# Mask of layer 3 added on VectorE with the row extremum, no mask products on TensorE, logits left in PSUM, all lists in a new order

## The reference

```
scores = einsum('bhqd,bhkd->bhqk', q, k) * scale
scores = where(adj == 0, -inf, scores)
attn = softmax(scores)
out = einsum('bhqk,bhkd->bhqd', attn, v) @ Wo.T + bo
```

## Time and profile before

| | us |
|---|---|
| median of 3 runs (lowest, highest) | 1394.55 (1393.59, 1395.53) |
| profiled execution, its own time | 1394.57 |
| its span in the trace | 1392.7 |
| mean granted TensorE clock, share of full | 0.994 |
| VectorE busy in TENSOR_REDUCE (L497, 256 of them) | 170.7 |
| VectorE busy in masked reductions (L450, 256) | 138.0 |
| ScalarE busy in layer 3's exponentials (L676, 1024) | 362.7 |

### The profile page before, as it was taken

How to read it: one execution, slowest core, us unless ns; L and a number is a source line. 1 busy time by engine, 2 the same in 40 slices (tenths; PEclk the granted TensorE clock), 3 DMA queues, 4 the chain that set the end, 5 groups by cost and what they waited for, 6 DMA issues and landing times. The chain is left out here.

```text
span 1392.7 us, 41293 instructions
## 1 busy us (share of the span) xinstructions
PE 1341.1 (96%) x12689; PEld 1173.4 (84%) x12689; DVE 1077.8 (77%) x3934; ACT 1006.3 (72%) x3905; POOL 918.3 (66%) x1225
## 2 busy tenths in 40 slices
PE   2799999999999999999999999999999999999986
PEld 2588888888888888888988888888888888898875
DVE  3787787787787788788778778778778778877853
ACT  0367777777777777777777777777777777777765
POOL 1577667677676776776776766767667677676543
PEclk9999999999999999999999999999999999999999
DMA  3001001101101001101000110110110110110000
GB/s 102 22 17 32 30 19 32 32 17 32 32 17 32 32 17 32 32 17 32 32 25 25 32 32 18 32 32 17 32 32 17 32 32 17 32 32 17 10 17 24
DMA packets 38888, 38.89 MB, mean 28 GB/s; under 512 B 3088, under 2 KB 38672, under 8 KB 38672
## 3 DMA queue, kind: packets, MB, share of 16 engines
q1 hardware_dynamic: 38672, 36.26, 8.5%
HBM read 19.47 MB, written 16.78 MB: 26 GB/s over the span
## 5 line engine op out<-in xcount | busy, mean ns | idle before, releaser
L301 POOL TENSOR_TENSOR probs<-exps,rsum 128x512 f32<-128x512 f32 x256 | 263.6, 1041 | 185.3 <-DVE rsum L504 185.3
L676 ACT ACTIVATE exps<-bank,nmax 128x128 f32<-128x128 f32 x1024 | 362.7, 383 | 1.7 <-DVE nmax L497 1.7
L441 DVE SCALAR_TENSOR_TENSOR ht_lo<-bank,ht_hi 128x512 fp32r<-128x512 f32 x192 | 130.8, 681 | 260.1 <-ACT ht_hi L614 260.1
L273 POOL TENSOR_TENSOR rstd<-veps,power 128x2 f32<-128x2 f32 x256 | 177.1, 692 | 212.8 <-DVE veps L412 212.7
L281 POOL TENSOR_SCALAR y<-x,nm,rstd 128x256 f32<-128x256 f32 x512 | 278.9, 554 | 33.0 <-issue 31.6
L684 ACT ACTIVATE probs3t<-bank 128x512 f32<-128x512 f32 x256 | 162.0, 634 | 103.1 <-PE bank L880 103.1
L676 ACT ACTIVATION_READ_ACCUMULATOR exps<-bank,nmax 128x1 f32 x1024 | 229.2, 224 | 0.0
L766 PE MATMUL bank<-w_hi,ht_hi 128*128 128x512 f32 (+1 forms) x512 | 185.9, 363 | 5.5 <-DVE ht_lo L441 5.4
L396 DVE BATCH_NORM_STATS2 stats<-x 128x6 f32<-128x256 f32 x512 | 186.7, 404 | 0.1
L768 PE MATMUL bank<-w_hi,ht_lo 128*128 128x512 f32 (+1 forms) x512 | 174.9, 342 | 0.0
L767 PE MATMUL bank<-w_lo,ht_hi 128*128 128x512 f32 (+1 forms) x512 | 174.3, 341 | 0.0
(11 more groups left out here) (121 smaller groups left out, 3786.7 us busy)
## 6 DMA issues: line engine op xcount, KB each, us to landing
x<-in_x SPq DMA_DIRECT2D x64, 256.0 KB, 2.8
out<-x SPq DMA_DIRECT2D x64, 256.0 KB, 3.1
w_sb<-in_w0t SPq DMA_DIRECT2D x1, 512.0 KB, 4.6
w_sb<-in_w SPq DMA_DIRECT2D x1, 256.0 KB, 5.2
w1t_sb<-in_w1t SPq DMA_DIRECT2D x1, 256.0 KB, 5.2
wq_sb<-in_wqt SPq DMA_DIRECT2D x1, 256.0 KB, 3.8
wk_sb<-in_wkt SPq DMA_DIRECT2D x1, 256.0 KB, 4.1
wv_sb<-in_wvt SPq DMA_DIRECT2D x1, 256.0 KB, 4.4
```

The lines of the kernel that those rows point to most:

```text
L273: pool.tensor_tensor(rstd[i][:, b], veps[i][:, b], power[:], ALU.pow).then_inc(S[f"rstd{i}"], 1)
L301: pool.tensor_tensor(probs3[:, p % BUFFERS["probs3"], j], exps3[:, p % BUFFERS["exps3"], j], rsum3[:, s, j].unsqueeze(2).to_broadcast([P, ...
L676: last = act.activation(exps3[:, b, j, i], bank_of(f"sc{j}")[:, i * P:(i + 1) * P], ACT.Exp, bias=nmax3[:, s, j, i:i + 1], accum_out=ssum3 ...
```

## The change

- The four mask products per pair go, with `start_scores`; `scores` begins its banks itself and now waits for all four.
- On VectorE `mask_scores` takes the place of `score_maximum`: per 128x128 score tile one TENSOR_TENSOR_REDUCE adds the mask, writes the negated sum to the new SBUF tile `masked3` (one buffer) and leaves its minimum in `nmax3`; four per bank, sixteen per pair. It waits for the exponentials of the pair before.
- `exps3_of` reads `masked3` with scale -1 in place of the bank. The score banks are freed by `nmax3_j`, no longer by `exp3_j`.
- `sum_logits` of layers 1 and 2 writes the logits into the other half of their PSUM bank, and `mask_logits` reads them there and writes `z`; the banks `d1` and `d2` are freed by `nmax1` and `nmax2`.
- The fp32 staging copies of six weights lie in `exps3` and `probs3`.
- The lags, the banks and the order of all four engines' lists are new. In the new table of lags the operations of each engine stand in the order of its new list.

The diff, cut to its core (the written-out lists of `step` follow the order of the new `LAG`; of `BANKS` the new table alone):

```
-       "load": -4, "store": 4, "e1t": 2, "qt_mm": 4, "x2_mm": 2, "mask3": 4, "e2t": 3, "mask1": 4, "scores": 4, "x3_mm": 3, "pt0": 5, "m1": 0,
-       "ot_mm": 5, "h1t": 1, "m0": 0, "x4_mm": 5, "v_mm": 4, "wh1_mm": 1, "wh0_mm": 1, "h2t": 2, "h3t": 3, "pt3": 4, "s0": 0, "pt2": 4, "d1": 1,
-       "hh_mm": 2, "kt_mm": 3, "d2": 2, "mask2": 3, "h0t": -1, "pt1": 4, "mask0": 3, "mj_hi0": 0, "exp3_0": 4, "wh1": 1, "exp3_1": 4, "wh0": 1,
-       "ht2": 2, "h3t_hi": 3, "v": 4, "p3t_2": 4, "z1": 1, "hh": 2, "p3t_3": 4, "exp1": 1, "z2": 2, "h0t_hi": -1, "at1": 1, "exp2": 2, "at2": 2,
-       "p3t_1": 4, "p3t_0": 4, "exp3_3": 3, "mj_hi1": -1, "ot_hi": 4, "h1t_hi": 0, "exp3_2": 3, "rsum3_0": 4, "stats1": 0, "kt": 3, "rsum1_any": 1,
-       "mv1": 0, "nmax2": 2, "veps1": 0, "h0t_lo": -1, "qt": 3, "rsum1": 1, "mv0": -2, "rsum2": 2, "x2": 1, "veps0": -2, "stats2": 1, "nmax3_3": 3,
-       "mv2": 1, "x3": 2, "veps2": 1, "nmax3_2": 3, "stats3": 2, "nmax3_0": 3, "mv3": 2, "t0_1": -1, "veps3": 2, "ot_lo": 4, "h1t_lo": 0,
-       "mj_lo1": -1, "rsum3_3": 3, "nmax3_1": 3, "mj_lo0": -1, "rsum3_2": 3, "t0_0": -1, "x4": 4, "h3t_lo": 2, "rsum3_1": 3, "stats0": -3, "x1": -1,
-       "nmax1": 0, "p3_1": 4, "x3_tail": 2, "p3_0": 4, "r3": 3, "rstd1": 0, "y1": 0, "rstd0": -2, "rstd2": 1, "y2": 1, "rstd3": 2, "y3": 2, "p3_3": 3,
-       "p3_2": 3, "y0": -2, "r0": -3,
+       "load": -4, "store": 5, "m1": 0, "pt3": 5, "v_mm": 4, "ot_mm": 5, "wh1_mm": 1, "wh0_mm": 1, "s0": 0, "h2t": 2, "d1": 1, "h0t": -1, "h3t": 3,
+       "pt2": 4, "x4_mm": 5, "hh_mm": 2, "kt_mm": 3, "e1t": 1, "d2": 2, "qt_mm": 3, "x2_mm": 1, "pt1": 4, "scores": 3, "m0": -1, "e2t": 2, "pt0": 4,
+       "h1t": 0, "x3_mm": 2, "p3t_0": 5, "mj_hi0": 0, "h1t_hi": 1, "exp3_3": 4, "mj_hi1": 0, "p3t_3": 5, "exp3_2": 4, "v": 4, "ot_hi": 5, "wh1": 1,
+       "wh0": 1, "z1": 1, "ht2": 2, "h3t_hi": 3, "h0t_hi": -1, "exp3_1": 4, "exp1": 1, "hh": 2, "at1": 1, "z2": 2, "exp3_0": 4, "exp2": 2, "p3t_2": 4,
+       "p3t_1": 4, "at2": 2, "stats2": 2, "nmax3_3": 4, "nmax3_0": 4, "mv2": 2, "nmax3_2": 4, "veps2": 2, "x3": 3, "h1t_lo": 1, "stats3": 3,
+       "mj_lo0": 0, "mv3": 3, "mj_lo1": 0, "veps3": 3, "t0_1": 0, "t0_0": 0, "nmax3_1": 4, "rsum3_2": 4, "ot_lo": 5, "x1": 0, "stats1": 0, "nmax1": 1,
+       "mv1": 0, "h3t_lo": 3, "veps1": 0, "h0t_lo": -1, "stats0": -3, "mv0": -3, "x4": 5, "rsum3_1": 4, "rsum1_any": 1, "kt": 3, "nmax2": 2, "qt": 3,
+       "rsum1": 1, "veps0": -3, "rsum3_0": 4, "x2": 1, "rsum3_3": 4, "rsum2": 2, "r0": -1, "rstd1": 1, "p3_1": 5, "x3_tail": 3, "y1": 1, "p3_0": 5,
+       "r3": 4, "rstd0": -2, "p3_3": 5, "rstd2": 2, "y2": 2, "rstd3": 3, "y3": 3, "p3_2": 4, "y0": -2,
 }
 
 
...
 BANKS = {
+    "m1": (4, "m1", ('mj_lo1', 't0_1')),
+    "pt3": (2, "pt3", ('p3t_3',)),
+    "v": (0, "v_mm", ('v',)),
+    "ot": (3, "ot_mm", ('ot_lo',)),
+    "wh1": (7, "wh1_mm", ('wh1',)),
+    "wh0": (0, "wh0_mm", ('wh0',)),
+    "x1b": (2, "s0", ('x1',)),
+    "h2t": (7, "h2t", ('ht2',)),
+    "d1": (5, "d1", ('nmax1',)),
+    "h0t": (6, "h0t", ('h0t_lo',)),
+    "h3t": (0, "h3t", ('h3t_lo',)),
+    "pt2": (4, "pt2", ('p3t_2',)),
+    "x4b": (3, "x4_mm", ('x4',)),
+    "hh": (2, "hh_mm", ('hh',)),
+    "kt": (5, "kt_mm", ('kt',)),
     "at1": (1, "e1t", ('at1',)),
+    "d2": (7, "d2", ('nmax2',)),
+    "qt": (0, "qt_mm", ('qt',)),
+    "x2b": (2, "x2_mm", ('x2',)),
+    "pt1": (7, "pt1", ('p3t_1',)),
+    "sc0": (3, "scores", ('nmax3_0',)),
+    "sc1": (1, "scores", ('nmax3_1',)),
+    "sc2": (0, "scores", ('nmax3_2',)),
+    "sc3": (5, "scores", ('nmax3_3',)),
+    "m0": (6, "m0", ('mj_lo0', 't0_0')),
+    "at2": (4, "e2t", ('at2',)),
+    "pt0": (2, "pt0", ('p3t_0',)),
     "h1t": (5, "h1t", ('h1t_lo',)),
+    "x3b": (7, "x3_mm", ('x3',)),
...
+        masked3 = sb("masked3", [P, BUFFERS["masked3"], HPC, DC * G, P])
...
+        w0_sb = probs3[:, 0, 0:2].rearrange("p j b n -> p (j b n)").rearrange("p (c o) -> p c o", o=D)
+        w1t_sb = probs3[:, 0, 2].rearrange("p b n -> p (b n)").rearrange("p (c o) -> p c o", o=D)
+        wq_sb, wk_sb, wv_sb, wo_sb = [exps3[:, 0, j].rearrange("p b n -> p (b n)").rearrange("p (c o) -> p c o", o=D) for j in range(HPC)]
...
             def mask_logits(i, msk, p):
                 b, s = p % BUFFERS[f"z{i}"], p % SMALL
                 passed(dve, f"z{i}", p)
                 passed(dve, f"exp{i}", p, SMALL)
-                for g in range(G):
-                    last = dve.tensor_tensor_reduce(z[i][:, b, g], z[i][:, b, g], msk[:], scale=-1.0, scalar=-MASKED, op0=ALU.add, op1=ALU.min,
+                read_before(dve, f"z{i}", p, f"exp{i}")
+                for g in range(G):
+                    last = dve.tensor_tensor_reduce(z[i][:, b, g], bank_of(f"d{i}")[:, (G + g) * P:(G + g + 1) * P], msk[:], scale=-1.0, scalar=-MASKED, op0=ALU.add, op1=ALU.min,
                                                     accum_out=nmax[i][:, s, g:g + 1])
                 last.then_inc(S[f"nmax{i}"], 1)
...
-            def score_maximum(j, p):
-                s = p % SMALL
+            def mask_scores(j, p):
+                b, s = p % BUFFERS["masked3"], p % SMALL
                 passed(dve, "scores", p)
-                passed(dve, f"exp3_{j}", p, SMALL)
-                dve.tensor_reduce(nmax3[:, s, j], bank_of(f"sc{j}")[:].rearrange("p (b n) -> p b n", n=P), AX.X, ALU.max,
-                                  negate=True).then_inc(S[f"nmax3_{j}"], 1)
+                passed(dve, f"exp3_{j}", p, BUFFERS["masked3"])
+                for i in range(DC * G):
+                    last = dve.tensor_tensor_reduce(masked3[:, b, j, i], bank_of(f"sc{j}")[:, i * P:(i + 1) * P], mask[:], scale=-1.0, scalar=-MASKED,
+                                                    op0=ALU.add, op1=ALU.min, accum_out=nmax3[:, s, j, i:i + 1])
+                last.then_inc(S[f"nmax3_{j}"], 1)
 
...
             def sum_logits(i, src, buffer, col, p):
-                b, bs = p % BUFFERS[f"z{i}"], p % BUFFERS[buffer]
+                bs = p % BUFFERS[buffer]
                 passed(act, f"d{i}", p)
-                read_before(act, f"z{i}", p, f"exp{i}")
-                for g in range(G):
-                    last = act.activation(z[i][:, b, g], bank_of(f"d{i}")[:, g * P:(g + 1) * P], ACT.Prelu, bias=src[:, bs, g, col:col + 1], alpha=SLOPE)
+                for g in range(G):
+                    last = act.activation(bank_of(f"d{i}")[:, (G + g) * P:(G + g + 1) * P], bank_of(f"d{i}")[:, g * P:(g + 1) * P], ACT.Prelu, bias=src[:, bs, g, col:col + 1], alpha=SLOPE)
                 last.then_inc(S[f"z{i}"], 1)
 
...
             def exps3_of(j, p):
                 for i in range(DC * G):
-                    last = act.activation(exps3[:, b, j, i], bank_of(f"sc{j}")[:, i * P:(i + 1) * P], ACT.Exp, bias=nmax3[:, s, j, i:i + 1],
+                    last = act.activation(exps3[:, b, j, i], masked3[:, p % BUFFERS["masked3"], j, i], ACT.Exp, bias=nmax3[:, s, j, i:i + 1], scale=-1.0,
                                           accum_out=ssum3[:, s, j, i:i + 1])
...
-            def start_scores(j, p):
-                bank_free(pe, f"sc{j}", p)
-                pe.matmul(bank_of(f"sc{j}")[:], ident_bf[:], mask_bf[:].unsqueeze(1).to_broadcast([P, DC * G, P]),
-                          start=True, stop=False).then_inc(S[f"mask{j}"], 1)
-
             def scores(p):
                 bq_, bk_ = p % BUFFERS["qt"], p % BUFFERS["kt"]
                 passed(pe, "qt", p)
                 passed(pe, "kt", p)
-
+                for j in range(HPC):
+                    bank_free(pe, f"sc{j}", p)
                 for c in range(DC):
                     for g in range(G):
                         for j in range(HPC):
                             r = slice(j * DH, (j + 1) * DH)
                             last = pe.matmul(bank_of(f"sc{j}")[:, (c * G + g) * P:(c * G + g + 1) * P], qt[r, bq_, c, g * P:(g + 1) * P],
-                                             kt[r, bk_, c, g * P:(g + 1) * P], start=False, stop=(c == DC - 1 and g == G - 1), tile_position=(j * DH, 0))
+                                             kt[r, bk_, c, g * P:(g + 1) * P], start=True, stop=True, tile_position=(j * DH, 0))
                 last.then_inc(S["scores"], 1)
 
```

More of the change, by code:

```diff
@@ L57 @@
[L57 to L71, removed]
@@ L310, in step @@
             def step(t):
+                if due(t, "r0"):
+                    biased_x0(t - LAG["r0"])
+                if due(t, "rstd1"):
+                    inverse_deviation(1, t - LAG["rstd1"])
                 if due(t, "p3_1"):
@@ L522, in step @@
             def step(t):
-                if due(t, "rsum3_0"):
-                    inverse_sum3(0, t - LAG["rsum3_0"])
+                if due(t, "stats2"):
+                    stats_of(2, x2, t - LAG["stats2"])
+                if due(t, "nmax3_3"):
+                    mask_scores(3, t - LAG["nmax3_3"])
+                if due(t, "nmax3_0"):
+                    mask_scores(0, t - LAG["nmax3_0"])
+                if due(t, "mv2"):
```

(81 more changed lines are left out.)

234 lines of the change are left out of this document (77 added, 157 removed).

## The result

| | before | after |
|---|---|---|
| median us (lowest, highest; 4 runs each) | 1394.07 (1393.25, 1395.53) | 1324.26 (1323.96, 1325.42) |
| span of the profiled execution | 1392.7 | 1323.6 |
| first addition of `x4` starts | 107.2 | 114.3 |
| distance of a pair in the middle (40 pairs) | 20.66 | 19.50 |

The changed kernel takes 0.9499 of the time before, 95% interval 0.9488 to 0.9511: 69.8 us less. The forecast was 1330.0, the range 1315 to 1375.

The account below looks back on a forecast made before the run. TensorE's sum of start-to-start distances was taken as the limit. Removing mask products saves 1.01 us per pair, 64.6 us over 64 pairs, other engines' additions staying hidden: 1394.57 - 64.6 = 1330.0 us, range 1315 to 1375.

Parts of the forecast that it names:

- What bounds the kernel: Middle stretch: TensorE, busy 826.00 of 826 us, sets the pace by its start-to-start distances, 20.65 us per pair.
- The 0.33 in front of the scores: TensorE's mask product before the scores: its extra 0.11 us is the change to quarter-array products; 0.10 given back.
- Mask products removed: TensorE: four products per pair cost 1.11 us, less 0.10 given back: 1.01 us per pair, 64.6 us saved.
- its bound of 55 us: Lower bound of the TensorE saving: 4 x 0.215 = 0.86 us per pair if every extra comes back elsewhere.
- Mask on VectorE: Twenty masked reductions from PSUM at 0.27 us replace older reductions: VectorE 16.57 to 17.58 us per pair, hidden under TensorE.
- the point from which VectorE decides: VectorE would set the pace from a masked-reduction distance of 0.37 us, and eat the whole gain from 0.42.
- Two operands in SBUF wait for GpSimd, one in PSUM with one in SBUF doesn't: VectorE's masked reductions: by this rule all twenty, with scores or logits in PSUM, would run undisturbed.
- ScalarE: Layer 3's 16 exponentials reading SBUF cost 0.88 us more per pair, 15.65 to 16.53, hidden at 84%.
- Rival A: Late hand-offs, at h1t (0.2 us spare) and wh0_mm (0.5), cost 0.3 to 0.7 us per pair: 1349 to 1375; chance 0.22.
- B: Masked reductions wait for GpSimd whatever their operands; VectorE sets the pace at 22.4 us per pair: 1506 us; chance 0.08.
- C: Layer 3's chain through single buffers closes a loop as long as the old period: 1394 us; chance 0.03.
- The new lists: All engines' orders: two close hand-offs fit by 0.2 and 0.5 us, others seem to have 0.7 or more; ends unchanged within 5.

Follow-up runs that it names:

- run 1: The kernel before with its four mask products per pair left out and nothing in their place, old lists: 1395.32 us, ratio 1.0004.
- run 5: The kernel before, mask products kept, with only the logits of layers 1 and 2 left in PSUM: 1377.13 us, ratio 0.9876.
- run 6: The kernel before without mask products and with the logits of layers 1 and 2 in PSUM, old order: 1341.55 us, ratio 0.9623.
- run 4: The changed kernel with the four mask products issued again in one block in front of the scores: 1383.30 us, period 20.42.
- run 3: The kernel before without mask products, layer 3's mask on VectorE, logits of layers 1 and 2 in PSUM, old lists: 1391.40 us, period 20.56.
- run 8: The changed kernel with each of layer 3's 16 masked reductions issued twice: 1425.76 us, period 20.96.
- run 9: The changed kernel with 8 of layer 3's 16 masked reductions issued twice: 1329.45 us, period 19.48.
- run 2: The kernel before without mask products, layer 3's mask on VectorE, logits of layers 1 and 2 still in SBUF, old order: 1449.58 us, ratio 1.039.
- run 62: Not a run of its own: "that run" is run 3, and 62 counts the veps instructions, of 256, that start while a GpSimd instruction runs.

## Why the prediction came out

The number and the sign were right. The reading of what bounds the kernel before was wrong, and that the saving came out whole was in part luck: it needed the new lists, and the sum has no term for them.

- **What bounds the kernel.** "The limit in the middle is the sum of PE's start-to-start distances" was wrong. Busy 826.00 of 826 looked like proof, but a product's row is longer than its distance (0.38 against 0.22 in the earlier trace rows) and covers a wait of up to 0.16 us behind it. Runs 1, 5 and 6 show that loop L set 20.66, TensorE's own sum being 20.4. The signs were there: the 0.29 and 0.27 in the earlier trace rows in front of transposes, the 0.28 from the transposes at 717.72 to the next product (0.21 in run 5), and both reductions ending on a GpSimd row. I took 0.12 us of this wait for all of it. The 0.33 in front of the scores I read rightly as the price of a change of tile: it is 0.31 in runs 4 and 5, where nothing waits there.
- **Mask products removed.** Forecast 1.01 us per pair, measured 1.15 in the period. It is made of 0.91 for the products (run 4 against the change; 0.89 in the forecast) and 0.25 for loop L, which the new order opens (runs 5 and 4; 0.12 in the forecast). The 58 and 16 us sum to 74; fill takes 7 us more (first `x4` at 114.3 in place of 107.2), the drain 4 less, as the spans have it: 63 x 1.153 = 72.6, less 7.2, plus 3.7: 69.1. I had left the ends at nothing. The forecast's own range ends at 1343; its bound of 55 us gives 1340.
- **Mask on VectorE.** A reduction from PSUM takes 0.21, my lower bound; taken was 0.27. VectorE's busy time is 729.97 / 42.35 = 17.24 us per pair against 17.58. It stays hidden, as said. But the rest of it is 17.24 - 20 x 0.21 = 13.0 and not 12.18. In run 3, with the same operations in the old lists, VectorE is busy 16.67 us per pair, so 0.57 of the 0.86 come with the new lists. Six idle gaps a pair in place of one long one leave more tails of instructions, and some got dearer (L425 476 ns, was 446 in the earlier trace rows); that these make the 0.57 is not shown. So the point from which VectorE decides, put at 0.37, is too high. By (19.50 - 13.0) / 20 it is 0.32, an estimate that fits runs 8 (20.5 us, over it) and 9 (18.7, hidden).
- **Two operands in SBUF wait for GpSimd, one in PSUM with one in SBUF doesn't.** Right, by 1280 reductions of at most 293 ns. Its weight was missed: I booked the end of this wait as VectorE load under cover, while in the old order it was on the path, 58 us between runs 2 and 3. The Trainium skill, "SBUF — State Buffer", section "Who interferes with whom", says that two SBUF inputs contend with a GpSimd instruction that reads SBUF; the reductions of all runs agree (up to 1399 ns with both operands in SBUF, at most 295 with one in PSUM). The prediction gave the other half too short: the section frees an instruction with at most one SBUF input only outside the 2-port perf modes. `veps` has one such input and did wait (last section); in which mode it ran no trace shows. By the Trainium skill, "VectorE: DVE Perf Modes", section on the TRN2 errata, an estimate for a reduction of 128 elements from PSUM is 258 ns (120 cycles and one per element at 0.96 GHz); the trace has a distance of 0.21 us, and the measurement decides.
- **ScalarE.** Four exponentials from `masked3` take 708.35 to 709.90 (rows below), 0.39 each: 16 x 0.05 = 0.8 us more by the distances, as forecast within 0.1. The busy time is 679.85 / 42.35 = 16.05 us per pair against 16.53, hidden: it rose by 0.4 alone, and where the other 0.4 went no run separates.

```profile
708.35 0.41 ACT L677 ACTIVATE exps<-masked,nmax 128x128 f32<-128x128 f32 x1
...
709.90 0.38 ACT L622 ACTIVATE mj_hi<-bank 128x256 fp32r<-128x256 f32 x1
```

- **Rival A** (late hand-offs) did not come: at `h1t` there is 1.0 us where I counted 0.2, since VectorE has run ahead and `nmax3_3` ends at 705.93; it doesn't appear with half a dose more (run 9), and with the whole dose as 0.3 us (run 8). **B** is out by the same 293 ns, **C** by the period of 19.50.
- **The new lists.** I looked in them for late hand-offs, and took the old ones, with no gap to be seen, as equally good. They weren't: the same operations in the old lists take 1391 us (run 3). That the exponentials come earlier before their transposes I had named, for 0.12 us; in fact the products' whole 0.91 hung on it as well (run 1: nothing).

What stays open: which moves in the lists open loop L. In the new ones the exponentials of layers 1 and 2 end about 0.6 and 2.3 us before their transposes start, but no run moved one operation alone.

## What to carry to other kernels

An engine that shows no gap is not thereby the bound: take a piece of its work away (here 1.1 us of 20.7) and see whether the period moves. Read its start-to-start distances too, in front of what depends on another engine, and set them beside those of the same instructions elsewhere. Where engines work in fixed lists, look for the loop that has no slack by following the idle times from engine to engine around one period; an edit that is worth nothing on one bound can be worth its whole length once the other is gone, so try edits in pairs as well. Put a list's load against the period by its busy time in the kernel at hand, and test the reserve with a dose of spare work.

## What I had not expected of the hardware

- Products that follow each other on TensorE show 0.00 idle while 0.25 us per pair of waiting is in their distances, and even with 1.1 us of work removed and the period unchanged only 29 of 826 us turned into visible idle time (796.78 busy in run 1).
- A masked reduction of 128x128 with accumulator costs the same distance from PSUM as undisturbed from SBUF, 0.21 us, though its row is 280 to 285 ns in both.
- In run 3 a small `veps` (128x2, SBUF to SBUF) that met a GpSimd instruction took 0.45 us in place of 0.15, so such instructions, with one operand in SBUF and the result there, can wait too. In that run 62 of 256 start while a GpSimd instruction runs and take 235 to 824 ns; the other 194 take at most 170:

```profile
713.87 0.45 DVE L411 TENSOR_SCALAR veps<-mv 128x2 f32<-128x2 f32 x1
714.23 0.16 DVE L412 TENSOR_SCALAR nm<-mv 128x2 f32<-128x2 f32 x1
```
